# Expert blocks of 64 rows in the two column halves of the array, and attention operands of 128 columns, in a graph-attention, attention and mixture-of-experts kernel

## The reference

```python
x = x + gnn(layernorm(x), edges)                 # two graph-attention layers
h = ln(layernorm(x)); q, k, v = h@Wq, h@Wk, h@Wv # 12 heads of 64
att = softmax(where(causal, q@k.T * 768**-0.5, -inf)); x1 = .. + (att@v)@Wp + bp
h2 = ln(x1); sel = argmax(h2 @ Wg)               # top-1 of 8; its softmax weight is 1
hid = relu(h2 @ W1[sel] + b1[sel])               # 768 -> 3072
y = hid @ W2[sel] + b2[sel]                      # 3072 -> 768
out = residual sum + y
```

## Time and profile before

| | us |
|---|---|
| median of 3 runs (1220.94 to 1224.35) | 1222.88 |
| profiled execution, its own time | 1224.95 |
| its span on the core | 1222.9 |
| PE / DVE / ACT / POOL busy | 1074.7 / 762.0 / 557.4 / 339.4 |
| first to last block of the experts | about 731 to 1216 |

### The profile page before, as it was taken

The page is one execution under the profiler, slowest core; times in us unless marked ns, Lnnn a source line. Parts: engine busy times, 40 slices in busy tenths (PEclk is TensorE's granted clock), DMA queues, the critical chain, the costliest instruction groups (busy, mean ns, idle before and its releaser), DMA issues.

```text
span 1222.9 us, 19243 instructions
## 1 busy us (share of the span) xinstructions
PE 1074.7 (88%) x6178; PEld 685.5 (56%) x6179; DVE 762.0 (62%) x1289; ACT 557.4 (46%) x740; POOL 339.4 (28%) x183
## 2 busy tenths in 40 slices
PE   5989688999699679999989408999999999999997
PEld 3555477546557446568877303545555555555554
DVE  7676678774536755358867418983112989889811
ACT  2676556303221134257642018683113777778511
POOL 3100000380003512034001327462000566566400
PEclk9999889999889879989999558999999999999999
DMA  8920200022401440020000289997001999999501
GB/s 295 370 72 1 103 1 1 1 103 76 78 1 64 78 78 1 1 100 2 2 2 1 62 194 378 340 372 262 13 26 32 352 376 375 364 386 363 214 16 28
DMA packets 98378, 170.63 MB, mean 140 GB/s; under 512 B 38611, under 2 KB 38691, under 8 KB 98330
## 3 DMA queue, kind: packets, MB, share of 16 engines
q1 hardware_dynamic: 88138, 145.33, 34.3%
q0 software_dynamic: 6016, 16.80, 4.5%
q10 hardware_dynamic: 4176, 7.87, 2.0%
HBM read 153.19 MB, written 18.79 MB: 141 GB/s over the span
## 4 chain that ended last, share of the span: by engine, by line
PE 66%; DVE 14%; issue 9%; POOL 4%; DMA 3%; ACT 2%; DVEq 1%; POOLq 0%; ACTq 0%; SPq 0%
PE psum L1329 32%; PE psum L1519 12%; PE psum L1540 12%; PE psum L1318 4%; DVE area L1270 3%; POOL area L635 2%; PE psum L1366 2%; DVE smalls L920 2%; DMA sorted_tokens<-area,smalls 1%; PE psum L1528 1%; DMA low<-in_L_ffn_W_dram 1%; DVE low L932 1%; DVE low L1036 1%; DVE low L1037 1%; PE psum L1381 1%
## 5 line engine op out<-in xcount | busy, mean ns | idle before, releaser
L1329 PE MATMUL psum<-area,low 128*125 128x256 f16 (+2 forms) x1080 | 250.4, 393 | 21.1 <-DVE low L1115 11.0
L1270 DVE TENSOR_TENSOR area<-low,area 128x1536 f16<-128x1536 f32 x96 | 231.9, 2456 | 18.9 <-ACT area L849 18.7
L635 POOL TENSOR_TENSOR area<-low,area 128x1536 f16<-128x1536 f32 x48 | 184.3, 3839 | 162.4 <-ACT area L849 162.3
L849 ACT ACTIVATE area<-low 128x1536 f16<-128x1536 f32 x144 | 209.5, 1482 | 36.0 <-DMA low<-in_L_ffn_W_dram 31.2
L1519 PE MATMUL psum<-area,low 128*128 128x512 f16 x972 | 221.4, 382 | 0.0
L1540 PE MATMUL psum<-area,low 128*128 128x384 f16 x1296 | 218.0, 326 | 2.3 <-DVE area L1270 1.1
L1329 PEld LDWEIGHTS psum<-area,low 128*125 128x125 f16 (+1 forms) x1080 | 151.2, 151 | 115.3 <-issue 64.0
L1329 PE MATMUL psum<-area 125*125 125x64 f16 (+9 forms) x1076 | 163.1, 304 | 12.2 <-DVE area L1256 8.0
L1540 PEld LDWEIGHTS psum<-area,low 128*128 128x128 f16 x1296 | 126.1, 98 | 82.7 <-issue 3.0
L1519 PEld LDWEIGHTS psum<-area,low 128*128 128x128 f16 x972 | 95.7, 98 | 114.1 <-issue 3.9
L1329 PEld LDWEIGHTS psum<-area 125*125 125x125 f16 (+2 forms) x1076 | 118.4, 160 | 42.0 <-issue 14.4
(11 more groups left out here) (202 smaller groups left out, 1239.7 us busy)
## 6 DMA issues: line engine op xcount, KB each, us to landing
low<-in_L_ffn_W_dram SPq DMA_DIRECT2D x144, 768.0 KB, 7.0
area<-in_L_gnn_W_dram SPq DMA_DIRECT2D x2, 3072.0 KB, 12.1
area<-in_L_gnn_Wr_dram SPq DMA_DIRECT2D x2, 3072.0 KB, 16.5
sorted_tokens<-area POOLq DMA_DIRECT2D x3, 1792.0 KB, 16.6
sorted_totals<-area POOLq DMA_DIRECT2D x3, 1792.0 KB, 28.8
low<-sorted_tokens ACTq DMA_DIRECT2D x11, 384.0 KB, 3.2
low<-sorted_totals ACTq DMA_DIRECT2D x9, 384.0 KB, 4.2
area<-in_L_ffn_Wv_dram SPq DMA_DIRECT2D x6, 384.0 KB, 6.3
```

The costliest lines, as they stand in the source:

```text
L635: pool.tensor_tensor(low_, raw_view(u), high_, ALU.subtract).then_inc(pool_low_ok, 1)
L849: act.activation(unit_parts(u)[0], raw_view(u), ACT.Copy).then_inc(high_ok, 1)
L1270: dve.tensor_tensor(low_, raw_view(u), high_, ALU.subtract).then_inc(dve_low_ok, 1)
L1329: ins = pe.matmul(place(name)[0:parts, at:at + w], left(q), right(q)[:, at:at + w], start=(q == 0), stop=(q == k - 1))
```

## The change

It has two parts.

Experts. A block has 64 rows (BR = 64), and there may be up to 17 blocks. Chunks are taken in pairs (C2 = 3). Each matmul has a stationary operand of 64 columns. In the first product the even chunk's result goes to PSUM partitions 0 to 63 and the odd chunk's to 64 to 127 of one bank; the bias product stays one matmul of 128 columns over a tile `picked` that ScalarE writes for each block. The relu and the transposes work on the pair as one 128-row tile. In the second product the two halves of the 768 outputs go to the two partition halves, so that the result is a tile of 128 partitions and 384 columns: half rows. Residual sums and ids are read as half rows (four DMAs for two), and the scatter writes half rows. Steps per block are 5 for 8. Conversions come in slices of four units: slices 0 and 1 run ahead (in steps 3 and 4 of an expert's last block), 2 after step 0, 3 after step 1, 4 and 5 after step 2. A product waits for all four units of its pair. Routing has ten thresholds for five.

Attention. The f16 operands that are loaded as weights (QT and the transposed attention weights) have 128 columns in place of 125; the three added ones are zeros or unused, and outputs have 128 partitions. Transposes are taken of 128 columns except the last.

```diff
-    BR = 128
-    NB = T + E - 1
+    BR = 64
+    NB = (N + E * (BR - 1)) // BR
+    C2, HD = C // 2, D // 2
...
-        UNITS = [(w, c, q) for s in range(1, C + 2) for w, c in ((1, s - 1), (2, s - 2)) if 0 <= c < C
-                 for q in range(2)]
+        UNITS = [(w, 2 * p + half, q) for s in range(1, C2 + 2) for w, p in ((1, s - 1), (2, s - 2)) if 0 <= p < C2
+                 for half in range(2) for q in range(2)]
...
-        AHEAD, PER_STEP = 3, U // (C + 2)
+        AHEAD, PER_SLICE = 2, 4
+        OWN, NEXT = {0: (2,), 1: (3,), 2: (4, 5)}, {3: (0,), 4: (1,)}
...
                 with eng.If(new_next > 0):
-                    for s_ in range(SPLIT, C + 2):
+                    for s_ in NEXT:
                         block_steps(b, e, s_)
-                        slice_(convert, a + 1, b + 1, s_ - SPLIT)
+                        for k in NEXT[s_]:
+                            slice_(convert, a + 1, b + 1, k)
...
+            def pick_bias(b):
+                e = act.value_load(tab[0:1, 0, bass.ds(b, 1)], min_val=0, max_val=E - 1)
+                act.activation(picked, b1_pick.rearrange("r (c e) -> r c e", c=C)[:, :, bass.ds(e, 1)].broadcast_to([112, C, BR]),
+                               ACT.Copy).then_inc(pick_ok, 1)
...
+                if s_ == C2:
+                    tokens_high(b + 1)
+                    pick_bias(b + 1)
+                    act.wait_ge(xt_used, b + 2)
+                    act.dma_start(xt, hs_dram[bass.ds(b * BR + 2 * BR, BR), :]).then_inc(xt_in, 16)
+                if s_ == C2 + 1:
...
-            for q in range(1, T):
+            for q in range(1, -(-N // BR)):
...
+                    product(("score", i), 3, lambda k: QT[h][PARTS[k][0]][:, t, :],
+                            lambda k: KT[PARTS[k][1]][:, h // 2, :], (t + 1) * P, 128)
...
+                    turn_scores(("attT", i - 2), t + 1, abuf[(i - 2) % ROWS])
...
                     for k in range(KD):
                         for x_, w_ in PARTS:
-                            ins = pe.matmul(psum[:, (c % 2) * BANK:(c % 2 + 1) * BANK], ht[x_][:, k, :],
-                                            w1_s[c][w_][:, k, :], start=False,
-                                            stop=(k == KD - 1 and x_ == 1))
+                            for half in range(2):
+                                ins = pe.matmul(psum[half * BR:(half + 1) * BR, p * BANK:(p + 1) * BANK], ht[x_][:, k, :],
+                                                w1_s[2 * p + half][w_][:, k, :], start=False,
+                                                stop=(k == KD - 1 and x_ == 1))
...
+                    for half in range(2):
+                        for j in range(CK):
+                            for x_, w_ in PARTS:
+                                for q in range(2):
+                                    ins = pe.matmul(psum[q * BR:(q + 1) * BR, 6 * BANK:6 * BANK + HD],
+                                                    hidT[p][x_][:, j, half * BR:(half + 1) * BR],
+                                                    w2_s[2 * p + half][w_][:, j, q * HD:(q + 1) * HD],
+                                                    start=(p == 0 and half == 0 and j == 0 and x_ + w_ == 0),
+                                                    stop=(p == C2 - 1 and half == 1 and j == CK - 1 and x_ == 1))
```

More of the change, by code:

```diff
@@ L383, in wait_split, with wait_pair, expert_blocks @@
                         a * len(mine) + (1 + back_) * len(mine) + mine.index(u) + 1)
-        def wait_chunk(eng, a, w, c):
-            wait_split(eng, a, unit_of[w, c, 1])
-            if (unit_of[w, c, 1] in POOL_UNITS) != (unit_of[w, c, 0] in POOL_UNITS):
-                wait_split(eng, a, unit_of[w, c, 0])
+        def wait_pair(eng, a, w, p):
+            units = [unit_of[w, 2 * p + half, q] for half in range(2) for q in range(2)]
+            wait_split(eng, a, [u for u in units if u not in POOL_UNITS][-1])
+            wait_split(eng, a, [u for u in units if u in POOL_UNITS][-1])
         HALVES = (slice(0, 64), slice(64, 128))
-        AHEAD, PER_STEP = 3, U // (C + 2)
-        assert U % (C + 2) == 0
+        AHEAD, PER_SLICE = 2, 4
+        OWN, NEXT = {0: (2,), 1: (3,), 2: (4, 5)}, {3: (0,), 4: (1,)}
         def slice_(convert, a, b, k):
-            for u in range(k * PER_STEP, (k + 1) * PER_STEP):
+            for u in range(k * PER_SLICE, (k + 1) * PER_SLICE):
                 convert(a, b, u)
-        def expert_blocks(eng, convert, first_tokens, block_steps, block_end):
+        def expert_blocks(eng, convert, first_tokens, block_steps, block_end=None):
             blocks = eng.value_load(nblocks[0:1, 0:1], min_val=1, max_val=NB)
@@ L605, in _ @@
                       allow_small_or_imprecise_dtypes=True).then_inc(consts, 1)
+            done(pool, ("QT", FC - 1))
+            pool.memset(A(4, 0, 2 * T * 128, P), 0.0).then_inc(zeroed, 1)
             for q in range(2):
@@ L637, in send_rows @@
             def send_rows():
-                pool.indirect_dma_start(out, bass.IndirectOffsetOnAxis(ap=ids, axis=0), y_o, None,
-                                        bounds_check=N - 1, oob_is_err=False).then_inc(y_out, 16)
+                pool.indirect_dma_start(out.rearrange("n (h d) -> (n h) d", h=2), bass.IndirectOffsetOnAxis(ap=ids, axis=0),
+                                        y_o, None, bounds_check=2 * N - 1, oob_is_err=False).then_inc(y_out, 16)
             pool.sem_inc(pool_low_ok, len(POOL_UNITS))
@@ L802, in _ @@
             n = T * FH
+            act.wait_ge(zeroed, 2)
             for i in range(n + 3):
@@ L1438, in _, with turn_scores @@
             n_ = T * FH
+            def turn_scores(name, k, tile):
+                free(pe, name)
+                for q in range(k):
+                    w = 128 if q < k - 1 else P
+                    ins = pe.transpose(place(name)[0:w, q * 128:q * 128 + P], tile[:, q * P:q * P + w], ident[0:P, 0:P])
+                ins.then_inc(made, 1)
             for i in range(n_ + 3):
@@ L1530, in turn_hidden, with second_product @@
                     ins.then_inc(hid_tr, 1)
-                def second_product(c):
-                    wait_chunk(pe, a, 2, c)
-                    pe.wait_ge(hid_relu, b * C + (c + 3))
-                    if c == 0:
+                def second_product(p):
+                    wait_pair(pe, a, 2, p)
+                    pe.wait_ge(hid_relu, b * C2 + (C2 + p + 1))
+                    if p == 0:
                         pe.wait_ge(y_cp, b + 1)
-                    for j in range(CK):
-                        for x_, w_ in PARTS:
-                            for q in range(2):
-                                ins = pe.matmul(psum[:, (4 + q) * BANK:(4 + q) * BANK + D // 2],
-                                                hidT[c % 2][x_][:, j, :],
-                                                w2_s[c][w_][:, j, q * D // 2:(q + 1) * D // 2],
-                                                start=(c == 0 and j == 0 and x_ + w_ == 0),
-                                                stop=(c == C - 1 and j == CK - 1 and x_ == 1))
+                    for half in range(2):
[7 more added lines that the diff above has]
+                                                    stop=(p == C2 - 1 and half == 1 and j == CK - 1 and x_ == 1))
@@ L1545, in second_product @@
                     ins.then_inc(hid_used, 1)
-                for s_ in range(C + 2):
-                    if s_ < C:
+                for s_ in range(C2 + 2):
+                    if s_ < C2:
                         first_product(s_)
-                    if 1 <= s_ <= C:
+                    if 1 <= s_ <= C2:
                         turn_hidden(s_ - 1)
-                    if s_ == 3:
+                    if s_ == 1:
                         turn_tokens(b + 1)
```

179 lines of the change are left out of this document (91 added, 88 removed).

## The result

| | before | after |
|---|---|---|
| median | 1223.21 (4 runs) | 1302.01 (4 runs, 1298.05 to 1304.49) |
| ratio to before, 95% interval | | 1.0644 [1.0622, 1.0666] |
| profiled execution, its own time / span | 1224.95 / 1222.9 | 1304.49 / 1302.2 |

The change costs 79 us where 18.5 were forecast. The direction was right; the size was four times too small and lies outside the range given.

The account below looks back on a forecast made before the run. In the expert stage TensorE and DMA end nearly together while weights load; TensorE alone is full when they are reused. Stage terms summed to +18.5 us: 1224.95 became 1243.5, less 2.1 for the median 1241.4; range 1208 to 1280.

Parts of the forecast that it names:

- The array: Expert blocks: two 64-column products side by side cost what one does; with switches a block takes 27 us (26 to 28).
- rival 2: Expert products: the halves do not overlap, a 64-row block costs about 51.3 us; about 1420 us, chance 0.08.
- rival 3: Expert products: a half's weight loads are not hidden, blocks about 37 us at worst; 1270 to 1330 us, chance 0.14.
- rival 1: Expert loads: raw buffers carry the DMA over ScalarE's wait, 48.5 us per expert; faster, 1209.6 us, chance 0.22.
- rival 4: Expert stage: break-even with free switches, warm clock, blocks of 26 and 51.3 us per expert; 1220 to 1226, chance 0.10.
- Restart: Last block of an expert: the next expert's first conversion comes 21.4 us into it, after the third turn.
- Weight loads: Expert loading: ScalarE's work 43.2 plus wait 7.2 gives 50.4, allowed 52.5 us per expert; first block done at 57.
- Clock: Loading stretches: two cold TensorE bursts per expert, up to 2.7 us each; half is already in 52.5 and 57.
- Attention and start: Attention's 128-column operands: -7 us (0 to -11), VectorE capping the last tiles; routing and first tokens: +1.3.
- Range: Whole kernel: 1208 to 1280 us, leaving out rival 2, most of rival 3 and the far end of rival 1.

Follow-up runs that it names:

- Run 4: The changed kernel with all 24 low parts subtracted on VectorE and none on GpSimd, conversion order unchanged: 1254.08 us, ratio 1.0239 to the kernel before.
- run 2: The changed kernel with conversion slice 4 directly after slice 3, ahead of the relu that waits for the third product: 1254.70 us, ratio 1.0266 to the kernel before.
- run 5: The changed kernel with both edits, slice 4 moved ahead (run 2) and all low parts on VectorE (run 4): 1212.68 us, ratio 0.9926 to the kernel before.
- run 11: The kernel of run 8 with four superfluous bias matmuls after each of units 11 to 14, inside the third product's wait: 1205.23 us, ratio 0.9855.
- run 8: The kernel of run 5 with three slices ahead and, in multi-block experts' last blocks, next slices 0, 1, 2 after steps 1, 3, 4: 1198.49 us, ratio 0.9778.
- run 1: The kernel before with only the attention part of the change (128-column operands): 1216.38 us, ratio 0.9941.

## Why the prediction was right or wrong

**The array.** Right. Two half-width products do run side by side. Start of the block that first reuses weights, after:

```profile
850.47 0.39 PE L1545 MATMUL psum<-low 112*128 112x512 f16 x1
850.78 4.08 PE L1550 MATMUL psum<-area,low 128*64 128x512 f16 x36
854.79 0.39 PE L1545 MATMUL psum<-low 112*128 112x512 f16 x1
```

Thirty-six matmuls take 4.08 where 18 took 4.05, and 48 of the second product take 4.09. The step from the bias to the product is 0.31 for 0.22, and a turn's 0.66 for 0.60: the switches are seen, at about 0.1 us each. Reuse blocks last 27.2, forecast 27 (26 to 28), where free switches give 26.0. With the drained switch of the Trainium skill (TensorEngine Tiling (Array Packing), Key Properties) the trace agrees in that each switch costs something; the upper end of 28, worked out from a drained matmul, was too much. Rivals 2 and 3 are refuted by these rows, 1 and 4 by the time.

**Restart.** Right: the next expert's first conversion comes 21.2 us into a last block, twice (932.06 to 953.29, 1151.14 to 1172.36), for 21.4.

**Weight loads.** Here the step failed: "On top comes the wait in which it can convert nothing: ... 7.2. Together 50.4". Two things were wrong in it.
- The size. The wait is 11.97, not 7.2: VectorE's lag behind the last conversion is 5.45 for 2.5 and the cold product 5.71 for 4.1; the bias row at half clock and gaps make up the rest. I had taken VectorE's mean of 2.46 as what a subtraction costs. It is a mean of 1.75 alone and up to 4.66 beside GpSimd in the kernel before; in the kernel after, 46 of 96 are stopped for 38 before, 30 of them at some 4.65 us for 13, and the mean rises to 2.996. Run 4 shows that GpSimd is the cause by taking it away. That the bursts of four conversions make the two engines meet more often is an argument; no run tried it.
- The form of the sum. I added ScalarE's work and its wait, 50.4, and compared it with the DMA's 49.8 as if the larger won. But a wait longer than the six buffers can cover stops the reads, and the time they lose comes on top of the 49.8. The DMA stands still for 4 us, and behind that the buffers come free with the low parts, some 3 us apart, where 24 units in 49.8 are 2.1 each. Runs 2 and 5 show it: with conversions running ahead of the waiting relu, the DMA is at 0.97, and with both cures an expert takes what its reads take.

The prediction had this hole in rival 1's "Against" (unit 22 cannot be read before 16 is split) and used it only against a gain; it had to be a rival of its own on the slow side, with the price of a stopped DMA. Measured per expert: 57 forecast for a first block became 68 to 74, and 52.5 for a period became 58.0 to 64.7.

**Clock.** The forecast counted two cold bursts per expert, with 2.7 in its terms and 5.4 at most. In the kernel after 20 products of six experts are cold, 3.3 per expert: they take 5.3 to 6.9 for 4.08, 38.7 us more in all or 6.4 per expert. How much of it is on the path is open; run 11 found nothing in the DMA-paced kernel, and run 8, the fastest of all, still has 11 cold products.

**Attention and start.** Attention alone: forecast -7, measured -6.5 by the medians, but that nearness is in part luck. In the traces the stage itself is 10.1 us shorter (run 1), and in the profiled execution 2.9 are given back between attention and the read of the first tokens (91.6 us for 88.6). The price of a narrow matmul was right: 15 of them behind the last scores take 0.60 us for 1.01, 27 ns less each. The last two tiles gave 7.0, under VectorE's cap of 8.4, and the first three another 3.1, for which the -7 for all tiles left no room.

The first conversion comes 13.5 earlier in the profiled execution, forecast 5.7, and 7.8 of this were missed. The last product before the experts starts 8.4 earlier (690.25 to 681.82): attention ends 10.5 earlier, and the longer routing chain takes back 1.6, as forecast (TensorE waits 9.64 for it, 8.02 before); half a microsecond more is lost on the way. The rest comes behind it: ScalarE's read of the first tokens is issued 10.4 earlier (704.42 for 714.77), it takes 10.7 to the first turned tile for 12.4, and that tile's operations are half as wide. Why the read is issued a further 2 us earlier was not tried.

**Range.** It ended at 1280. Only a rival for the stopped reads, which it lacked, could have carried it to 1302.

## What to carry to other kernels

Where an engine that feeds a ring of buffers also stands in the chain of products, count how long it can wait before the ring is full: in this kernel the wait was free up to there, and beyond it the reads stood still and their lost time came on top. One slice of work ahead of the waiting instruction was worth 47 us here. Look at the least and the most of an operation's duration, not its mean: a mean of 2.46 us was 1.75 alone and up to 4.66 beside GpSimd, and a third of the work moved onto the busier engine made it less busy. Here smaller blocks paid only once the loads restarted early, since blocks that reuse weights leave the DMA idle; with the order, the engine and the restart mended, blocks of 64 rows took 1198.5 us against 1206.6 for the best with 128 (0.978 and 0.988 of the kernel before). An earlier restart was not tried with blocks of 128 rows, so how much of these 8 us belongs to the block's size is open.

## What the runs showed of the hardware that was not expected

- Two operands in SBUF on VectorE beside a subtraction on GpSimd: 5.2 us at most instead of 1.75 in the kernel after, and 8.0 at most in run 2, across two of GpSimd's. Every lengthened one ends 1.6 us after a GpSimd subtraction. Without GpSimd all 144 lie between 1744 and 1760 ns.
- Switching between half-width and full-width matmuls costs about 0.1 us a switch (an estimate: 27.2 less 26.0 for some 11 switches).
- A weight load of 64 columns is not shorter than one of 128: 116 to 122 ns on average after, 98 before (the pages' groups). The pairs of products keep the full-width pace all the same.
- Matmuls put between the arriving units kept the granted clock at its full level (2.4 GHz) up to the product (4.08); after one burst of 5.35 us and then 8.82 us of idle time it began at the lower one (6.02).
- A stationary operand of 128 columns in place of 125 makes attention 81.9 us long for 92.0, and then VectorE holds most of the chain in the last row tile. The kernel's median gains 6.5.
